# A recurrent pipeline over four engines: one sum and the shifted variances on VectorE, a new order on TensorE and ScalarE, two buffers for a tanh

## The chip, the core and the metric

The program runs on one core of a Trainium2 chip. The core has TensorE (PE in the profile) for matrix products and transposes, VectorE (DVE), ScalarE (ACT) and GpSimd (POOL) for the rest, and queues that start DMAs. Each engine runs its own list of instructions in order, and the lists meet only at semaphores. The metric is the time of one whole execution on the device, in microseconds, and less is better.

## What is computed

The program is a chain of four sub-layers on 32 sequences of 256 tokens with 128 features, in float32. The change lies in the third, which is a recurrent mixing layer followed by a gated feed-forward layer:

```python
def _wkv(k, v, time_decay, time_first):       # a scan along the tokens
    ew = jnp.exp(-jnp.exp(time_decay))
    def step(carry, kv):
        a, b = carry
        ek = jnp.exp(kv[0])
        a = ew * a + ek * kv[1]
        b = ew * b + ek
        return ((a, b), a / (b + WKV_EPS))
...
xn = _ln(x, ln1_g, ln1_b)
xp = _shift(xn)                               # the token before
k = (xn * mix_k + xp * (1.0 - mix_k)) @ Wk
v = (xn * mix_v + xp * (1.0 - mix_v)) @ Wv
r = jax.nn.sigmoid((xn * mix_r + xp * (1.0 - mix_r)) @ Wr)
wkv = _wkv(k, v, time_decay, time_first)
x = x + r * wkv @ Wo
yn = _ln(x, ln2_g, ln2_b)
yp = _shift(yn)
kk = jnp.square(jax.nn.relu((0.5 * yn + 0.5 * yp) @ Wfk))
rr = jax.nn.sigmoid(yn @ Wfr)
return x + rr * (kk @ Wfv)
```

The layer's input is a normalised sum of the sub-layer before, whose expert outputs are gathered by token here, and its own output is added to `x` and normalised again. `_ln` needs a mean and a variance over the 128 features of each token.

## The kernel before

`build` runs the stages one after the other, each in a block of its own that ends on all engines before the next begins. The change is in `recur` (L1645), which takes the 32 sequences, called t, through a pipeline of stages. Every engine has the same loop `for i in turns` (i from -3 to 39), and in turn i it works on several sequences at once, each a fixed number of turns older: in the middle of the stage GpSimd gathers for i+3, VectorE sums and measures i+1, TensorE turns i, the scans work on i-1, `output` on i-2, the second normalisation on i-3, `keys` on i-4 and `values` on i-5. `live(t)` says whether a sequence is in 0 to 31. The order of an engine's work in a turn is the order of the calls in its loop, written by hand. `wait_past(engine, semaphore, n)` waits where n is positive.

What a turn does on each engine, in its order before the change:

- TensorE (L1791): `keys(i-4)` multiplies `both` by `w_k` in eight matmuls into two `key_bank`s; `project(i-1)` makes key and value in `kv_bank` and the first gate in the left half of `gate_bank` from `xn`; `output(i-2)`; `turn(i)` transposes `z` once it is there; `turn_second(i-3)` transposes `z2`; `values(i-5)`; `receptance(i-4)` makes the second gate in the right half of `gate_bank`.
- ScalarE (L1888): `exponents(i-1)` writes `e_k` from the key bank; `normalise_second(i-3)` and `normalise_first(i)` write `z2` and `z` with the scales in `roots` and the offsets in `shifts`; `rectify(i-4)` reads the key banks; `affine_second(i-3)` writes `yn`; `add_eps(i-1)` writes `b_eps`; `gate(i-1)` is the first tanh; `square(i-4)`; `affine(i)` writes `xn`; `normalise_row(i)`; `normalise_third(i-7)` writes `fresh`; `gate_second(i-4)` is the second tanh, into the one buffer `half_tanh2`.
- VectorE (L2042): `shift(i-1)` writes `shifts` once GpSimd has made `roots`; then means and variances of `total` (`aggregate(2)`), `weigh` (`ekv`), the two gathered sums, the two scans, `add_output`, the spreads, the reciprocal (L1996), the last `moments` (two `aggregate`s, four instructions at L1947), `double` (L2026), `gate_second` (L2015), `divide` (L2002), `add_second` (L2022), `gate` (L2008) and the spread of `total` (L1941).
- GpSimd (L2116): two gathers, `add_old(i-3)` (L2113), which writes `both` as the sum of `yn` and `yn` one token earlier, a third gather, `scale(i)` and the fourth gather. `scale` waits for the `moments` of the turn, adds the epsilons to the variances in two small instructions (`bases`, L2104 and L2105) and raises ten numbers a partition to the power -1/2 (`roots`, L2108).

The semaphores that matter: `moments_done` lets `scale` begin, `rooted` lets `shift` begin, `shifted` lets ScalarE normalise, `both_ready` lets `keys` begin, `yn_ready` lets `both` be made, `gated2_done` frees `half_tanh2` and half of `out_bank`.

## Time and profile before

| what | value |
|---|---|
| median of 3 runs | 2475.6 us (2472.62 to 2476.64) |
| the profiled execution | 2475.63 us |
| its span, first to last instruction | 2473.9 us |
| granted TensorE clock, mean of the span | 0.891 |
| the recurrent stage | 1214 to 1549 us |
| a turn in its middle | 8.96 us |
| busy over the span: PE, DVE, ACT, POOL | 79%, 62%, 52%, 42% |

In a row of a timeline the first number is the start, the second the length, and a bracket at the end gives the idle time of that engine before it and what ended it. Two instructions of the same kind that follow each other are one row with x2. The lengths of neighbours overlap a little, so what an instruction costs its engine is the distance to the next start. Instructions that start DMAs or only wait are not counted as busy, except GpSimd's indirect gathers.

### The profile page before, as it was taken

Reading aid. Unit: us, or ns where it says so; the run is one execution under the profiler, and the core shown is the slowest. Engines: PE = TensorE matmul, PEld = TensorE weight load, DVE = VectorE, ACT = ScalarE, POOL = GpSimd, SP = SyncE. Lnnn points to the kernel's source line nnn. Section 1 sums busy time; section 2 is a strip of 40 time slices with the busy share of each in tenths; the row PEclk is TensorE's granted clock in tenths of the full one; section 3 lists DMA queues with packets and bytes.
Section 4 is the critical chain, followed back from the end, with each engine's and each line's share of the span. In section 5 each row is a group of like instructions: output and inputs, shape, how many; then the busy total and the mean of one; then the engine's idle time right before and its main releaser. Section 6 shows DMA issues by size and latency. Waiting matters only on the chain. (4 is left out here: it accounts for less than half of the span.)

```text
span 2473.9 us, 52699 instructions
## 1 busy us (share of the span) xinstructions
PE 1946.5 (79%) x16756; PEld 1600.7 (65%) x16788; DVE 1531.0 (62%) x6215; ACT 1275.3 (52%) x3105; POOL 1046.7 (42%) x1285
## 2 busy tenths in 40 slices
PE   7799999999997897999578888599998758856610
PEld 6455555555555886877467777488887757755500
DVE  2478788888886583421279997588887564313345
ACT  3588888888884322333258887344443104423310
POOL 2133333333331315555478885222222115566654
PEclk9799999999998898999889999799999559977655
DMA  7799999999995104555412221000001115533323
GB/s 237 254 313 311 312 311 317 313 311 312 312 313 164 56 1 124 154 154 151 108 29 58 60 60 44 18 1 2 1 1 30 74 34 155 155 114 110 101 73 74
DMA packets 198092, 353.95 MB, mean 143 GB/s; under 512 B 25280, under 2 KB 145856, under 8 KB 196800
## 3 DMA queue, kind: packets, MB, share of 16 engines
q1 hardware_dynamic: 140752, 294.77, 36.6%
q0 software_dynamic: 17664, 36.21, 6.2%
q10 hardware_dynamic: 39408, 19.60, 2.7%
q8 instruction: 143, 2.34, 0.4%
q14 instruction: 125, 1.02, 0.1%
HBM read 165.87 MB, written 145.52 MB: 126 GB/s over the span
## 5 line engine op out<-in xcount | busy, mean ns | idle before, releaser
L1389 POOL DMA_INDIRECT moe_route_rows_sb<-tokens,moe_taken x296 | 279.8, 945 | 291.7 <-PE moe_route_bank L1429 145.6
L177 POOL TENSOR_SCALAR_AFFINE_SELECT heads_raw_relative<-heads_raw_relative 128x508 f32<-128x508 f32 x256 | 166.7, 675 | 500.8 <-ACT heads_raw_relative L562 460.9
L1547 DVE COPY moe_route_y<-moe_route_bank 128x128 f32<-128x128 f32 x296 | 86.1, 291 | 427.3 <-PE moe_route_bank L1448 218.9
L1488 ACT COPY moe_route_rows_t<-moe_route_bank 128x128 f32<-128x128 f32 x296 | 78.4, 265 | 435.0 <-PE moe_route_bank L1429 270.1
L1438 PE MATMUL moe_route_bank<-moe_route_rows_t,moe_route_w_now 128*128 128x128 f32 x1184 | 220.9, 315 | 85.7 <-issue 74.9
L562 ACT COPY heads_raw_relative<-heads_rel_bank 128x768 f32<-128x768 f32 x247 | 198.7, 804 | 125.6 <-PE heads_rel_bank L457 125.5
L1448 PE MATMUL moe_route_bank<-moe_w,moe_route_hid 128*128 x1184 | 218.9, 312 | 47.3 <-issue 24.8
L486 PE MATMUL attend_turn_bank<-ident,attend_score 128*128 128x128 f32 x1536 | 232.0, 287 | 20.5 <-ACT attend_prob_t L568 19.2
L1438 PEld LDWEIGHTS moe_route_bank<-moe_route_rows_t,moe_route_w_now 128*128 128x128 f32 x1184 | 180.3, 217 | 103.8 <-issue 98.9
L486 PEld LDWEIGHTS attend_turn_bank<-ident,attend_score 128*128 128x128 f32 x1536 | 163.8, 142 | 117.5 <-ACT attend_prob_t L568 68.1
L568 ACT ACTIVATE attend_prob_t<-attend_turn_bank 128x384 f32<-128x384 f32 x512 | 224.8, 500 | 6.9 <-PE attend_turn_bank L486 6.9
L1448 PEld LDWEIGHTS moe_route_bank<-moe_w,moe_route_hid 128*128 128x128 f32 x1184 | 175.2, 212 | 72.4 <-issue 65.8
L572 ACT ACTIVATE attend_score<-attend_score,attend_extreme 128x128 f32<-128x128 f32 x512 | 215.7, 421 | 9.1 <-DVE attend_extreme L619 8.8
L619 DVE CUSTOM_DVE_ANT_0 attend_score<-attend_score_bank,heads_relative 128x256 f32<-128x256 f32 x512 | 214.5, 419 | 0.0
L625 DVE TENSOR_SCALAR attend_score<-attend_score,attend_extreme 128x256 f32<-128x256 f32 x512 | 195.2, 381 | 0.0
L616 DVE CUSTOM_DVE_ANT_0 attend_score<-attend_score_bank,heads_relative 128x128 f32<-128x128 f32 x512 | 146.2, 285 | 78.4 <-PE attend_score_bank L457 52.6
L2229 POOL TENSOR_TENSOR batch_prob<-batch_e_x,batch_recip 128x512 f32<-128x512 f32 x64 | 67.1, 1048 | 234.4 <-DVE batch_recip L2446 234.4
L457 PE MATMUL attend_score_bank<-heads_qk 32*128 32x256 f32 x1024 | 156.1, 381 | 0.0
L457 PE MATMUL heads_rel_bank<-heads_e,heads_qk 32*128 32x256 f32 x988 | 150.8, 382 | 0.0
L2092 POOL DMA_INDIRECT recur_got<-expert_out,moe_slots x128 | 136.8, 1068 | 32.1 <-issue 32.1
L1382 POOL DMA_INDIRECT moe_route_got<-expert_out,moe_slots x128 | 121.7, 951 | 65.2 <-issue 40.9
L454 PE MATMUL heads_rel_bank<-heads_e,heads_qk 32*128 32x128 f32 x988 | 122.9, 325 | 21.2 <-PEq L59 3.2
(321 smaller groups left out, 5072.4 us busy)
## 6 DMA issues: line engine op xcount, KB each, us to landing
shear<-heads_raw_relative SPq DMA_DIRECT2D x128, 768.0 KB, 5.5
heads_relative<-shear SPq DMA_DIRECT2D x128, 768.0 KB, 6.4
moe_route_w_now<-moe_w SPq DMA_DIRECT2D x296, 129.0 KB
expert_out<-moe_route_y ACTq DMA_DIRECT2D x73, 256.0 KB
qk_heads<-project_qk SPq DMA_DIRECT2D x32, 256.0 KB, 4.3
heads_qk<-qk_heads SPq DMA_DIRECT2D x128, 64.0 KB
tokens<-moe_z SPq DMA_DIRECT2D x8, 1024.0 KB, 4.1
moe_route_rows_sb<-tokens,moe_taken POOLq DMA_INDIRECT x296
```

The costliest lines, as they stand in the source:

```text
L177: m = nc.gpsimd.affine_select(out=future, in_=future, compare_op=ALU.is_ge, fill=-BIG, base=1 - P, pattern=[[0, QUAD], [1, P - 1]], channe ...
L457: mm = nc.tensor.matmul(bank[:, P:W], q[:, P:T], m[:, P:W] if of_rel else m[:, 0:T], start=True, stop=True)
L486: mm = nc.tensor.transpose(bank[:, j * P:(j + 1) * P], score[:, (h - LAG) % RING, j * P:(j + 1) * P], c.ident[:, :])
L562: nc.scalar.copy(raw[:, ring, 2 * half:2 * half + 2, :], r_bank[:, :, 0:W]).then_inc(rel_moved, 1)
L568: nc.scalar.activation(prob_t[:, (h - LAG) % RING, :], bank_of(h)[:, 0:W], ACT.Exp).then_inc(exped, 1)
L572: nc.scalar.activation(score[:, h % RING, 0:P], score[:, h % RING, 0:P], ACT.Identity, bias=extreme[:, h % RING, 0:1], scale=-1.0).then_in ...
L616: nc.vector.tensor_tensor_reduce(score[:, row, 0:P], bank[:, 0:P], rel[:, quad, h % QUAD, 0:P], -SM_SCALE, 3.0e38, ALU.add, ALU.min, extre ...
L619: nc.vector.tensor_tensor_reduce(score[:, row, P:W], bank[:, P:W], rel[:, quad, h % QUAD, P:W], SM_SCALE, -3.0e38, ALU.add, ALU.max, extre ...
L625: nc.vector.tensor_scalar(score[:, h % RING, P:W], score[:, h % RING, P:W], extreme[:, h % RING, 1:2], None, ALU.subtract).then_inc(centre ...
L1389: nc.gpsimd.indirect_dma_start(rows_sb[:, s % TAKEN, :], None, c.tokens, bass.IndirectOffsetOnAxis(ex.taken[:, s // S, s % S:s % S + 1], 0 ...
L1438: mm = nc.tensor.matmul(hid_bank[u][:, k * P:(k + 1) * P], w1_now[r][:, k * P:(k + 1) * P], rows_t[u][:, :], start=True, stop=True)
L1448: mm = nc.tensor.matmul(y_bank[:, 0:D], hid[u][:, k, :], w, start=k == 0, stop=k == 1)
```

## The change

Four things change, all in `recur`.

`add_old` moves from GpSimd to VectorE, behind `divide`. The two instructions for `bases` move to VectorE as `shift_variances`, behind `double`, and `scale` on GpSimd now waits for them and makes only `roots`. On VectorE `gate_second` also moves, from behind `double` to behind `gate`, directly ahead of `add_second`. On TensorE `keys` moves from the head of the turn to behind `output`, and on ScalarE the first tanh and `add_eps` move ahead of `rectify`, the tanh first. `half_tanh2` gets two buffers. The semaphore `halved` takes over the start-up part of `based`.

```diff
-        half_tanh2, gated2 = sb("half_tanh2", [P, T]), sb("gated2", [P, T])
+        half_tanh2, gated2 = [sb(f"half_tanh2_{u}", [P, T]) for u in range(2)], sb("gated2", [P, T])
...
             for i in turns:
-                if live(i - 4):
-                    keys(i - 4)
                 if live(i - 1):
                     project(i - 1)
                 if live(i - 2):
                     output(i - 2)
+                if live(i - 4):
+                    keys(i - 4)
                 if live(i):
                     turn(i)
...
             def gate_second(t):
                 act.wait_ge(r2_made, t + 1)
-                wait_past(act, gated2_done, t)
-                nc.scalar.activation(half_tanh2[:, :], gate_bank[:, T:2 * T], ACT.Tanh, scale=0.5).then_inc(tanhed2, 1)
+                wait_past(act, gated2_done, t - 1)
+                nc.scalar.activation(half_tanh2[t % 2][:, :], gate_bank[:, T:2 * T], ACT.Tanh, scale=0.5).then_inc(tanhed2, 1)
...
                 if live(i):
                     normalise_first(i)
+                if live(i - 1):
+                    gate(i - 1)
+                    add_eps(i - 1)
                 if live(i - 4):
                     rectify(i - 4)
                 if live(i - 3):
                     affine_second(i - 3)
-                if live(i - 1):
-                    add_eps(i - 1)
-                    gate(i - 1)
...
+            def add_old(t):
+                dve.wait_ge(yn_ready, t + 1)
+                wait_past(dve, k_made, 2 * t - 2)
+                nc.vector.tensor_tensor(both[t % 2][:, :], yn[t % 2][:, 1:], yn[t % 2][:, 0:T], ALU.add).then_inc(both_ready, 1)
+
+            def shift_variances(turn):
+                u = turn % 2
+                dve.wait_ge(moments_done, moments_made(turn))
+                wait_past(dve, rooted, scales_made(turn - 2))
+                nc.vector.tensor_scalar(bases[u][:, 0:3, :], moments[u][:, :, :, 1], 1.0, LN_EPS, ALU.mult, ALU.add)
+                nc.vector.tensor_scalar(bases[u][:, 3:5, :], moments[u][:, 0::2, :, 1], 1.0 + LN_EPS, LN_EPS ** 2, ALU.mult, ALU.add
+                                        ).then_inc(based, 1)
...
                 if live(i - 5):
                     double(i - 5)
-                    gate_second(i - 5)
+                if i in scaled:
+                    shift_variances(i)
                 if live(i - 1):
                     divide(i - 1)
-                if live(i - 5):
-                    add_second(i - 5)
+                if live(i - 3):
+                    add_old(i - 3)
                 if live(i - 1):
                     gate(i - 1)
                 if live(i - 5):
+                    gate_second(i - 5)
+                    add_second(i - 5)
                     dve.wait_ge(totalled, i - 4)
                     spread(2, i - 5, total[(i - 5) % SUMS])
...
             def scale(i):
                 u = i % 2
-                pool.wait_ge(moments_done, moments_made(i))
+                pool.wait_ge(halved, 1)
+                pool.wait_ge(based, scales_made(i))
...
-                nc.gpsimd.tensor_scalar(bases[u][:, 0:3, :], moments[u][:, :, :, 1], 1.0, LN_EPS, ALU.mult, ALU.add).then_inc(based, 1)
-                nc.gpsimd.tensor_scalar(bases[u][:, 3:5, :], moments[u][:, 0::2, :, 1], 1.0 + LN_EPS, LN_EPS ** 2, ALU.mult, ALU.add
-                                        ).then_inc(based, 1)
-                pool.wait_ge(based, 2 * scales_made(i) + 1)
                 nc.gpsimd.tensor_tensor(roots[u][:, :, :], bases[u][:, :, :], minus_half[:, :, :], ALU.pow).then_inc(rooted, 1)
...
-            def add_old(t):
-                pool.wait_ge(yn_ready, t + 1)
-                wait_past(pool, k_made, 2 * t - 2)
-                nc.gpsimd.tensor_tensor(both[t % 2][:, :], yn[t % 2][:, 1:], yn[t % 2][:, 0:T], ALU.add).then_inc(both_ready, 1)
...
-                if live(i - 3):
-                    add_old(i - 3)
```

TensorE, a turn in the middle of the stage; `key_bank` is written by `keys`, `kv_bank` by `project`, `out_bank` by `output` (L1751) and `values` (L1787), `turn_bank` by the two transposes:

```order
 L1743 MATMUL recur_gate_bank<-recur_xn,recur_w_old 128x256
 L1751 MATMUL recur_out_bank<-recur_w_out,recur_gated 128x128 x2
+L1767 MATMUL recur_key_bank<-recur_both,recur_w_k 128x256 x4
 L1730 MATMUL recur_turn_bank<-ident,recur_z 128x128 x2
 L1759 MATMUL recur_turn_bank<-ident,recur_z 128x128 x2
 L1787 MATMUL recur_out_bank<-recur_w_v,recur_kk 128x128 x8
 L1777 MATMUL recur_gate_bank<-recur_w_r,recur_yn 128x128 x2
-L1767 MATMUL recur_key_bank<-recur_both,recur_w_k 128x256 x4
 L1742 MATMUL recur_kv_bank<-recur_xn,recur_w_now 128x256
```

`keys` has gone from ahead of the projections to behind `output`, ahead of the transpose that waits for `z`.

VectorE before, from the reciprocal to the `shifts` of the next turn; `recur_gated` at L2015 is the second gate, at L2008 the first:

```order
L1996 RECIPROCAL recur_b_inv<-recur_b_eps 128x256
L1947 BN_AGGR recur_moments<-recur_stats 128x2 x4
L2026 TENSOR_TENSOR recur_total<-recur_x_2,rows 128x256
L2015 SCALAR_TENSOR_TENSOR recur_gated<-recur_half_tanh,recur_out_bank 128x256
L2002 TENSOR_TENSOR recur_ratio<-recur_scan_a,recur_b_inv 128x256
L2022 TENSOR_TENSOR recur_total<-recur_total,recur_gated 128x256
L2008 SCALAR_TENSOR_TENSOR recur_gated<-recur_half_tanh,recur_ratio 128x256
L1941 BN_STATS recur_stats<-recur_total 128x6 x2
L1953 SCALAR_TENSOR_TENSOR recur_shifts<-recur_moments,recur_roots 128x6
```

VectorE now, the same stretch (line numbers are those of the changed kernel; L2028 is the second gate, L2021 the first):

```order
L2009 RECIPROCAL recur_b_inv<-recur_b_eps 128x256
L1947 BN_AGGR recur_moments<-recur_stats 128x2 x4
L2039 TENSOR_TENSOR recur_total<-recur_x_1,rows 128x256
L1988 TENSOR_SCALAR recur_bases<-recur_moments 128x6
L1989 TENSOR_SCALAR recur_bases<-recur_moments 128x4
L2015 TENSOR_TENSOR recur_ratio<-recur_scan_a,recur_b_inv 128x256
L1982 TENSOR_TENSOR recur_both<-recur_yn 128x256
L2021 SCALAR_TENSOR_TENSOR recur_gated<-recur_half_tanh,recur_ratio 128x256
L2028 SCALAR_TENSOR_TENSOR recur_gated<-recur_half_tanh_1,recur_out_bank 128x256
L2035 TENSOR_TENSOR recur_total<-recur_total,recur_gated 128x256
L1941 BN_STATS recur_stats<-recur_total 128x6 x2
L1953 SCALAR_TENSOR_TENSOR recur_shifts<-recur_moments,recur_roots 128x6
```

The two `bases` and `both` are new in the row, and the second gate now stands directly ahead of the add that reads it.

GpSimd before, a turn:

```order
L2108 TENSOR_TENSOR recur_roots<-recur_bases,recur_minus_half 128x10
L2092 DMA recur_got<-expert_out,moe_slots 128x128 x3
L2113 TENSOR_TENSOR recur_both<-recur_yn 128x256
L2092 DMA recur_got<-expert_out,moe_slots 128x128
L2104 TENSOR_SCALAR recur_bases<-recur_moments 128x6
L2105 TENSOR_SCALAR recur_bases<-recur_moments 128x4
```

GpSimd now, two turns and the start of a third:

```order
L2121 TENSOR_TENSOR recur_roots<-recur_bases,recur_minus_half 128x10
L2108 DMA recur_got<-expert_out,moe_slots 128x128 x4
L2121 TENSOR_TENSOR recur_roots<-recur_bases,recur_minus_half 128x10
L2108 DMA recur_got<-expert_out,moe_slots 128x128 x4
L2121 TENSOR_TENSOR recur_roots<-recur_bases,recur_minus_half 128x10
```

Only the gathers and `roots` are left there.

## Rows read from the trace of the kernel before

**Rows 1.** By stretch: busy us (instructions) of PE, PEld, DVE, ACT, POOL; then granted clock.
```profile
1380.00:1420.00 40.00, 36.01 (x212) 31.85 (x213) 35.98 (x135) 32.62 (x80) 33.97 (x37) 1.00 0.26 60
```

**Rows 2.** Waits, 1262 to 1500 us: who waited for whom, us in total, times, longest.
```profile
ACT recur_e_k L1825 <- PE recur_kv_bank L1743: 42.5, 26, 4.6
...
DVE recur_shifts L1953 <- POOL recur_roots L2108: 23.6, 26, 2.2
...
DVE recur_ekv L1972 <- ACT recur_e_k L1826: 2.6, 2, 1.3
```

**Rows 3.** Timeline of VectorE, one turn; start, length, instruction, idle before.
```profile
1392.89 0.17 DVE L1953 SCALAR_TENSOR_TENSOR recur_shifts<-recur_moments,recur_roots 128x6 f32<-128x6 f32 x1 [0.81 <-POOL recur_roots L2108]
1392.97 0.16 DVE L1955 SCALAR_TENSOR_TENSOR recur_shifts<-recur_moments,recur_roots 128x2 f32<-128x2 f32 x1
...
1398.68 0.32 DVE L1947 BATCH_NORM_AGGREGATE recur_moments<-recur_stats 128x2 f32<-128x6 f32 x4
1398.91 0.39 DVE L2026 TENSOR_TENSOR recur_total<-recur_x,rows 128x256 f32<-128x256 f32 x1
1399.22 0.41 DVE L2015 SCALAR_TENSOR_TENSOR recur_gated<-recur_half_tanh,recur_out_bank 128x256 f32<-128x256 f32 x1
...
1399.89 0.43 DVE L2022 TENSOR_TENSOR recur_total<-recur_total,recur_gated 128x256 f32<-128x256 f32 x1
1400.24 0.41 DVE L2008 SCALAR_TENSOR_TENSOR recur_gated<-recur_half_tanh,recur_ratio 128x256 f32<-128x256 f32 x1
1400.57 0.47 DVE L1941 BATCH_NORM_STATS2 recur_stats<-recur_total 128x6 f32<-128x128 f32 x2
1401.85 0.17 DVE L1953 SCALAR_TENSOR_TENSOR recur_shifts<-recur_moments,recur_roots 128x6 f32<-128x6 f32 x1 [0.80 <-POOL recur_roots L2108]
```

**Rows 4.** Timeline of GpSimd, the same turn.
```profile
1397.12 0.62 POOL L2113 TENSOR_TENSOR recur_both<-recur_yn 128x256 f32<-128x256 f32 x1
...
1399.09 0.28 POOL L2104 TENSOR_SCALAR recur_bases<-recur_moments 128x6 f32<-128x6 f32 x1 [0.23 <-DVE recur_moments L1947]
...
1399.72 2.10 POOL L2108 TENSOR_TENSOR recur_roots<-recur_bases,recur_minus_half 128x10 f32<-128x10 f32 x1
```

**Rows 5.** Timeline of TensorE, the same turn and the next.
```profile
1397.79 2.00 PE L1767 MATMUL recur_key_bank<-recur_both,recur_w_k 128*128 128x256 f32 x8
1399.62 0.59 PE L1742 MATMUL recur_kv_bank<-recur_xn,recur_w_now 128*128 128x256 f32 x2
...
1403.82 0.44 PE L1730 MATMUL recur_turn_bank<-ident,recur_z 128*128 128x128 f32 x2 [1.00 <-ACT recur_z L1817]
```

**Rows 6.** Timeline of ScalarE, the turn after.
```profile
1401.55 0.26 ACT L1825 ACTIVATE recur_e_k<-recur_kv_bank,recur_cols 128x1 f32<-128x1 f32 x1 [1.44 <-PE recur_kv_bank L1743]
...
1402.12 0.88 ACT L1817 ACTIVATE recur_z<-recur_x,recur_shifts,recur_roots 128x128 f32<-128x128 f32 x2
...
1406.69 0.56 ACT L1874 ACTIVATE recur_xn<-recur_turn_bank,recur_cols 128x256 f32<-128x256 f32 x1
```

**Rows 7.** Timeline of VectorE, tail of the stage.
```profile
1530.83 0.42 DVE L2015 SCALAR_TENSOR_TENSOR recur_gated<-recur_half_tanh,recur_out_bank 128x256 f32<-128x256 f32 x1 [3.16 <-issue]
1531.29 0.42 DVE L2022 TENSOR_TENSOR recur_total<-recur_total,recur_gated 128x256 f32<-128x256 f32 x1
1531.75 0.48 DVE L1941 BATCH_NORM_STATS2 recur_stats<-recur_total 128x6 f32<-128x128 f32 x2
```

**Rows 8.** The line that makes roots; ns shortest/median/longest, first and last start us.
```profile
L2108 POOL TENSOR_TENSOR recur_roots<-recur_bases,recur_minus_half x39: 1952/2094/2104, 1230.2 to 1545.5; 128x10 f32<-128x10 f32 x39
```

**Rows 9.** Timeline of GpSimd, first and last steady turn, one of the tail.
```profile
1283.44 2.10 POOL L2108 TENSOR_TENSOR recur_roots<-recur_bases,recur_minus_half 128x10 f32<-128x10 f32 x1
...
1498.48 2.10 POOL L2108 TENSOR_TENSOR recur_roots<-recur_bases,recur_minus_half 128x10 f32<-128x10 f32 x1
...
1534.78 0.61 POOL L2113 TENSOR_TENSOR recur_both<-recur_yn 128x256 f32<-128x256 f32 x1 [3.24 <-ACT recur_yn L1853]
...
1536.03 1.96 POOL L2108 TENSOR_TENSOR recur_roots<-recur_bases,recur_minus_half 128x10 f32<-128x10 f32 x1
```

More of the change, by code:

```diff
@@ L1685, in recur @@
         stats_done = [sem(f"stats_done{k}") for k in range(3)]
-        half_summed, summed, row_ready, moments_done, based, rooted, shifted, ratio2_done, rest_done = (
-            sem(x) for x in ("half_summed", "summed", "row_ready", "moments_done", "based", "rooted", "shifted", "ratio2_done", "rest_done"))
+        half_summed, summed, row_ready, moments_done, based, halved, rooted, shifted, ratio2_done, rest_done = (
+            sem(x) for x in ("half_summed", "summed", "row_ready", "moments_done", "based", "halved", "rooted", "shifted", "ratio2_done", "rest_done"))
         gathered = c.indirect["moe0_gathered"]
@@ L2014, in gate_second @@
                 wait_past(dve, totalled, t)
-                nc.vector.scalar_tensor_tensor(out=gated2[:, :], in0=half_tanh2[:, :], scalar=1.0, in1=out_bank[:, T:T + BLK * D],
+                nc.vector.scalar_tensor_tensor(out=gated2[:, :], in0=half_tanh2[t % 2][:, :], scalar=1.0, in1=out_bank[:, T:T + BLK * D],
                                                op0=ALU.add, op1=ALU.mult).then_inc(gated2_done, 1)
@@ L2103, in scale @@
                 wait_past(pool, rest_done, upto(i - 8))
-                nc.gpsimd.tensor_scalar(bases[u][:, 0:3, :], moments[u][:, :, :, 1], 1.0, LN_EPS, ALU.mult, ALU.add).then_inc(based, 1)
-                nc.gpsimd.tensor_scalar(bases[u][:, 3:5, :], moments[u][:, 0::2, :, 1], 1.0 + LN_EPS, LN_EPS ** 2, ALU.mult, ALU.add
-                                        ).then_inc(based, 1)
-                pool.wait_ge(based, 2 * scales_made(i) + 1)
                 nc.gpsimd.tensor_tensor(roots[u][:, :, :], bases[u][:, :, :], minus_half[:, :, :], ALU.pow).then_inc(rooted, 1)
-            def add_old(t):
-                pool.wait_ge(yn_ready, t + 1)
-                wait_past(pool, k_made, 2 * t - 2)
-                nc.gpsimd.tensor_tensor(both[t % 2][:, :], yn[t % 2][:, 1:], yn[t % 2][:, 0:T], ALU.add).then_inc(both_ready, 1)
-            nc.gpsimd.memset(minus_half[:, :, :], -0.5).then_inc(based, 1)
+            nc.gpsimd.memset(minus_half[:, :, :], -0.5).then_inc(halved, 1)
             for i in turns:
```

## The prediction

> **What bounds the kernel now.** The change touches only the recurrent stage, from 1214 to 1549 us of a span of 2473.9 us. The stage is a block of its own, so what it loses or gains counts in full. I read the busy table by stretch first [rows 1]: in the middle of the stage all four engines are 82 to 90% busy and TensorE's granted clock is 1.00. Nothing is far ahead, so a ring of waits sets the period of a turn. The list of waits over 26 turns [rows 2] shows that each waits for another once a turn: ScalarE 1.6 us on the mean for the key and value projections, VectorE 0.9 for `roots`. The timelines say which of these is the ring.
>
> VectorE [rows 3]: `shifts` starts at 1392.89 and again at 1401.85, a period of 8.96. Between them VectorE works to the spread of `total`, which starts 7.68 in, then waits 0.80 for `roots`. The last `moments` end at 1399.00. GpSimd [rows 4]: the two `bases` start at 1399.09, `roots` at 1399.72, and `roots` ends at 1401.82, 0.03 before `shifts`. So the ring is: VectorE from `shifts` to the end of `moments` 6.11, wake 0.09, `bases` 0.63, `roots` 2.10, wake 0.03, together 8.96. Two others lie close behind. GpSimd alone is idle 0.23 before `bases`, so it could turn in about 8.75. For TensorE and ScalarE [rows 5, 6]: TensorE idles 1.00 for `z` ahead of `turn`, so its own work is 7.96; ScalarE starts `z` 0.57 after `e_k` (two instructions), about 0.1 later than instructions of that length need, which is the slack of that ring.
>
> **What leaves the ring.** The two `bases` leave GpSimd, 0.63 a turn, and `both` too, 0.62 and what stands behind it [rows 4]. GpSimd then needs about 7.6 a turn and is no bound. Against that, VectorE now runs `double` and the two new instructions before `roots` can start. Back to back, a VectorE instruction costs 0.07 to 0.09 less than its length: `shifts` is 0.17 long and its successor starts 0.08 later, `add_second` 0.43 long and the next starts 0.35 later [rows 3]. So `double`, 0.39 long, costs 0.31. The new two have 6 and 4 elements a partition, and no row shows them on VectorE. The nearest is `shifts`, same engine and size: 0.08 a step, 0.15 to 0.17 long [rows 3]. On GpSimd they took 0.28 and together 0.63 [rows 4], the dear end. I take 0.08 each, the row of the same engine. The ring becomes 6.02 to the start of `double`, 0.31, 0.08, 0.15 for the second to end, wake 0.09, `roots` 2.10, wake 0.03: 8.78.
>
> **What fills VectorE.** Its work before is 7.68 to the last spread and 0.40 for it: 8.08. Added are the two small ones, 0.16, and `both`, a 128x256 add of two SBUF inputs, whose like are `double` at 0.31 and `add_second` at 0.35 [rows 3], so 0.33 (0.62 on GpSimd is the other end [rows 4]). The new order also puts three dependent instructions in a row: second gate, add, spread. In the tail of the stage the same three run so, with steps of 0.46 and 0.46 [rows 7]; in the middle of the old order the second gate costs 0.33 and the add 0.35 [rows 3]: 0.24 more. The sum is 8.08 + 0.16 + 0.33 + 0.24 = 8.81. That is just above the ring: VectorE itself is late next, and the period is **8.81** against 8.96.
>
> One rule speaks against exactly this move. Rows first: `add_second` at 1399.89 and `gate` at 1400.24 each read two SBUF tensors, start while `roots` (1399.72 to 1401.82) reads SBUF on GpSimd, and take 0.43 and 0.41, about as much as `double` at 0.39, which runs before `roots` [rows 3, 4]. The Trainium skill (SBUF — State Buffer, Who interferes with whom) says that such a pair exclude each other: whoever starts second is blocked until the other ends. By the rows the sum stands at 8.81 a turn; by that rule it would be the lock rival below, 10.74.
>
> **The new order on TensorE and ScalarE** gives nothing by itself in the middle, but the move needs it. `both` now starts 6.8 after `shifts` (6.33 to the small ones, 0.16, divide 0.34) and ends at 7.2; `keys` began at 1397.79, 4.9 after `shifts`, and `project` at 1399.62 [rows 5]. With `keys` still ahead, the projections would wait 2.3. In the new order TensorE projects as soon as `xn` is there: ScalarE has the same instructions between `z` and `xn`, so `xn` is done 5.1 after `z` starts (1402.12 to 1406.69 and 0.56) [rows 6], 5.4 after `shifts`. Projections, gate and `output` take 3.2 (1399.62 to 1403.82 less 1.00), so to 8.6; `keys` take 1.83 more (1397.79 to 1399.62), to 10.5, that is 1.7 into the next turn, while `z` is done at 1.97 of it (1403.82 against 1401.85). So 0.2 to 0.3 remains of TensorE's 1.0 idle. The key and value banks are made 1.9 after `project` starts (1399.62 to `e_k` at 1401.55), at 7.3, and ScalarE's own work ends at about 7.2. ScalarE gets `keys` late as well; it fills the time with the first tanh and `b_eps` and rectifies at about 2.5, by when half of `keys` is made. `add_old` makes VectorE wait for `yn`, with `gate`, the second gate, spread and `shifts` queued behind it; `yn` comes before `xn`, so before 5.4, and is asked for at 6.8. The second `half_tanh2` buffer lets ScalarE write the next tanh while VectorE's second gate, now later, reads the last one; with one buffer `e_k` would stand behind that wait. The cover of all this is VectorE's full row.
>
> **The stage's turns.** `roots` runs 39 times, from 1230.2 to 1545.5, so there are 38 intervals [rows 8]: 6 of ramp up to 1283.44 (53.3 us), 24 steady to 1498.48 (215.0 us, 8.96 each) and 8 of tail (47.1 us) [rows 9].
> Steady: 24 x 0.15 = **3.6** us.
> Ramp: in the first four intervals the `bases` go from GpSimd's chain, 0.63 [rows 4] against about 0.1 to 0.2 on VectorE; I count 0.5 each, 2.0. The last two are the longest, 10.2 and 9.9: there `keys` stands before `project`, and VectorE waits for `e_k` twice, 2.6 in all, 1.3 at most [rows 2]. With `project` ahead those 1.3 go, and 0.45 of `bases`: 1.75 each, 3.5. Ramp: **5.5**, between 2 (only `bases`) and 7.
> Tail: once no gathers are left, `roots` queues on GpSimd behind `both`, which waits 3.24 for `yn`: from the start of `both` at 1534.78 to `roots` at 1536.03 are 1.25 [rows 9]. In the new order `roots` does not wait for `both`. I count 1.25 for two intervals and 0.3 for the three before them, 3.4; the last three may grow as `values` catch up, and I take 0.4 back. Tail: **3.0**, between 0 and 5.
> Sum: 3.6 + 5.5 + 3.0 = **12.1**. The profiled execution took 2475.63 us with a span of 2473.9, the same as the median of the runs, so the sum is taken from 2475.6: **2463.5 us**. With the terms at their ends (steady 0 to 5 by the price of the small ones) it is 2458.6 to 2473.6.
>
> **Rivals.**
> *VectorE is full already.* If its additions cost 0.15 more a turn (0.16 each for the small ones do that), the steady turn stays 8.96 and ramp and tail alone gain 8.5: 2467. For: VectorE is within hundredths of the ring, and no row shows it reading `moments` in steps. Against: `shifts` reads them so. 15%.
> *Ramp and tail give little.* The first turns wait on something else than `keys`, and in the tail `values` takes the place of `both`: 2, 0 and steady 2 to 3, 2471. Against: the 2.6 of waiting for `e_k` is in the trace. 10%.
> *The moved instructions keep GpSimd's price* (slower). VectorE would pay 0.63 for the small ones and 0.78 for `both` with its wait, 0.92 more than I charged: a turn of 9.73, 24 x 0.77 = 18.5 lost, 8.5 gained in ramp and tail: 2485.6. It decides from 0.15 extra a turn, turns the sign at 0.5 and passes 0.2% at 0.7. Every VectorE row of the two sizes speaks against. 9%.
> *The lock.* `both`, at 6.83, would be held by `roots` to 8.76, and after it run `gate`, second gate, add and spread: 0.33 + 0.33 + 0.46 + 0.46 + 0.40, a turn of 10.74; 24 x 1.78 = 42.7 lost and 8.5 back, 2509.8. The 0.43 and 0.41 above speak against. 3%. This is the rule of the Trainium skill named above.
> *More than forecast.* `roots` shrinks from 2.10 to the 1.95 of its shortest [rows 8] and VectorE hides the dependent steps: 8.65 a turn, tail 5: 2457.6. 8%.
> The forecast keeps 55%.
>
> **How the numbers follow.** A measurement of this kernel tells 0.2%, about 5 us, from no change. Faster by more: the forecast, the last case, most of the first and a little of the second, 0.74. Within: 0.14. Slower: the third and fourth, 0.12. The range 2457 to 2474 leaves out those 0.12 and about 0.06 of still larger gains.
>
> **What would show it.** In the profile after: `roots` to `roots` 8.81 in the middle; VectorE's wait for `roots` from 0.8 to under 0.1; steps of 0.08 for the small ones and 0.46 from second gate to add and to spread; GpSimd idle about 1.1 before `roots`; TensorE's wait for `z` 0.2 to 0.3; no wait of `ekv` for `e_k` in the ramp. I am wrong if VectorE waits for `yn`, if TensorE waits for `both`, or if `both` or `gate` lasts over 0.5 under `roots`.

## The result and the profile after

| | before | changed |
|---|---|---|
| median of 19 runs each | 2475.6 us (2469.38 to 2487.28) | 2481.65 us (2471.99 to 2491.88) |
| profiled execution, its span | 2475.63, 2473.9 us | 2483.72, 2482.0 us |
| first to last `roots`, 38 turns | 315.4 us | 318.6 us |
| a turn in the middle | 8.96 us | 9.44 us |

The ratio is 1.0028, 95% interval 1.0018 to 1.0037: slower by 0.3%, where 12 us of gain were forecast. The stage lost 3.2 us in the profiled executions. The other 4.9 us of the two spans lie mostly behind the last `roots` (933.0 against 928.3 us), almost all of it in stages that were not changed; a second profile of the changed kernel, below, has 929.4 there. So 3.2 is what the change did, and the rest of the 6 us between the medians has no place in the code that these runs show.

The line that makes `roots`, answering [rows 8] (ns shortest/median/longest, first and last start in us):

```profile
L2121 POOL TENSOR_TENSOR recur_roots<-recur_bases,recur_minus_half x39: 1954/2702/2713, 1230.4 to 1549.0; 128x10 f32<-128x10 f32 x39
```

The median has gone from 2.09 to 2.70 us, with the same instruction, operands and engine. Its shortest is still 1.95. The timeline of VectorE and GpSimd together, one turn in the middle, answering [rows 3, 4] (start, length, engine, instruction, idle before):

```profile
1390.50 0.32 DVE L1947 BATCH_NORM_AGGREGATE recur_moments<-recur_stats 128x2 f32<-128x6 f32 x4
1390.73 0.39 DVE L2039 TENSOR_TENSOR recur_total<-recur_x,rows 128x256 f32<-128x256 f32 x1
1391.04 0.16 DVE L1988 TENSOR_SCALAR recur_bases<-recur_moments 128x6 f32<-128x6 f32 x1
1391.11 0.16 DVE L1989 TENSOR_SCALAR recur_bases<-recur_moments 128x4 f32<-128x4 f32 x1
1391.18 0.42 DVE L2015 TENSOR_TENSOR recur_ratio<-recur_scan_a,recur_b_inv 128x256 f32<-128x256 f32 x1
1391.41 2.70 POOL L2121 TENSOR_TENSOR recur_roots<-recur_bases,recur_minus_half 128x10 f32<-128x10 f32 x1 [1.22 <-issue]
1391.52 0.42 DVE L1982 TENSOR_TENSOR recur_both<-recur_yn 128x256 f32<-128x256 f32 x1
1391.85 0.42 DVE L2021 SCALAR_TENSOR_TENSOR recur_gated<-recur_half_tanh,recur_ratio 128x256 f32<-128x256 f32 x1
1392.19 0.41 DVE L2028 SCALAR_TENSOR_TENSOR recur_gated<-recur_half_tanh,recur_out_bank 128x256 f32<-128x256 f32 x1
1392.63 0.42 DVE L2035 TENSOR_TENSOR recur_total<-recur_total,recur_gated 128x256 f32<-128x256 f32 x1
1393.09 0.49 DVE L1941 BATCH_NORM_STATS2 recur_stats<-recur_total 128x6 f32<-128x128 f32 x2
1394.15 0.17 DVE L1953 SCALAR_TENSOR_TENSOR recur_shifts<-recur_moments,recur_roots 128x6 f32<-128x6 f32 x1 [0.57 <-POOL recur_roots L2121]
```

Read the starts: the small instructions cost 0.07 each, `both` 0.33 (1391.52 to 1391.85), the second gate 0.44 and the add 0.46, all as forecast. None of VectorE's instructions under `roots` is longer than 0.42. Only `roots` is long, and VectorE idles 0.57 for it. The ring is now 6.02 + 0.31 + 0.07 + 0.30 (1391.11 to 1391.41, of it 0.14 of wake) + 2.71 + 0.03 = 9.44.

The waits of 1262 to 1500 us, answering [rows 2] (who waited for whom, us in total, times, longest):

```profile
ACT recur_z L1817 <- DVE recur_shifts L1955: 39.9, 26, 1.7
...
PE recur_turn_bank L1730 <- ACT recur_z L1817: 18.2, 24, 0.8
...
DVE recur_shifts L1953 <- POOL recur_roots L2121: 15.5, 25, 1.2
ACT recur_e_k L1825 <- PE recur_kv_bank L1743: 12.4, 26, 3.1
```

The first three hang on the ring: VectorE waits 0.6 a turn for `roots`, ScalarE 1.5 for `shifts`, TensorE 0.8 for `z`. The wait of `ekv` for `e_k`, 2.6 before, is gone, and in this stretch no engine waits for `both` or `yn`.

By stretch of the stage: the ramp's six turns take 47.6 us (53.3 before), the 24 of the middle 226.1 (215.0), the tail's eight 44.8 (47.1). That is 5.6 and 2.2 won and 11.1 lost. The length of `roots` goes with it: 1.99 to 2.04 in the ramp, 2.70 or 2.71 in 23 turns of the middle (2.41 and 2.16 in two), 1.95 to 2.01 in the late tail.

### The profile page after: what moved, and what is told of

It reads as the page before. It is cut to its first block and busy times, and to the rows that moved or that the text cites. A ratio compares the mean times of both kernels' runs of the same rounds, so it can differ in the third digit from the quotient of the medians.

```text
span 2482.0 us, 52771 instructions
## 1 busy us (share of the span) xinstructions
PE 1950.0 (79%) x16756; PEld 1594.0 (64%) x16788; DVE 1553.7 (63%) x6325; ACT 1276.8 (51%) x3105; POOL 1025.2 (41%) x1175
## 3 DMA queue, kind: packets, MB, share of 16 engines
q8 instruction: 143, 2.34, 0.4%
```

## Experiments

The expectations call the explanations by letters. P: `roots` is held back while VectorE runs instructions with two SBUF inputs one behind the other. L: it is long because VectorE is busy during all of it (the load). W: it is long because GpSimd has idled and wakes, or because VectorE has just written its operands. T, which comes later: any run of full-size VectorE instructions holds it, and only something about the second gate ends that. "The small two" are the two `bases`.

The experiments are told in the order in which they ran. Each edit is against the changed kernel unless it says otherwise. The table has the length of `roots` and the turn in the middle, the 38 turns, and the ratio to the kernel before, with its interval where there were several runs. The first four ran on a chip on which the kernel before took 2352.5 us, so their times compare only as ratios; the turns of the stage compare all the same, since the one with the old GpSimd and VectorE code has 8.96 and 2.10 there too.

| experiment | `roots` | turn | 38 turns | ratio to before |
|---|---|---|---|---|
| second gate first | 1.98 | 8.72 | 303.0 | 0.9939 (0.9924 to 0.9954) |
| `both` back on GpSimd | 2.04 | 8.77 | 302.2 | 0.9934 (0.9920 to 0.9949) |
| `bases` back on GpSimd | 1.98 | 8.96 | 311.0 | 0.9985 (0.9975 to 0.9995) |
| orders only | 2.10 | 8.96 | 311.5 | 0.9981 (0.9972 to 0.9990) |
| changed kernel again | 2.71 | 9.44 | 318.5 | 1.0016 (1.0000 to 1.0032) |
| hide and shorten | 1.98 | 8.68 | 302.7 | 0.9954 (0.9936 to 0.9972) |
| longer run | 2.03 | 8.88 | 304.8 | 0.9966 (0.9948 to 0.9984) |
| pause of 32 | 2.04 | 8.78 | 303.3 | one run: 2464.14 against 2472.06 us |
| pause of 96 | 2.08 | 8.81 | 303.1 | one run: 2456.05 against 2474.56 us |
| `both` from one input | 2.03 | 8.77 | 303.7 | one run: 2459.36 against 2474.56 us |
| keys ahead | 2.70 | 11.22, 12.89 | 401.9 | 1.0354 (1.0332 to 1.0376) |
| one tanh buffer, pause of 32 | 2.04 | 8.78 | 306.5 | one run: 2466.1 against 2474.56 us |
| first gate from one input | 2.37 | 9.10 | 310.4 | one run: 2469.15 against 2472.53 us |
| second gate from two inputs | 3.04 | 9.78 | 327.0 | one run: 2483.7 against 2472.53 us |

**Second gate first.** It is the one whose bank operand lies in PSUM; it now stands between the `bases` and `divide`.

```diff
                     shift_variances(i)
+                if live(i - 5):
+                    gate_second(i - 5)
                 if live(i - 1):
                     divide(i - 1)
...
                 if live(i - 5):
-                    gate_second(i - 5)
                     add_second(i - 5)
```

> The changed kernel with one call moved: on VectorE the second gate runs directly behind the two small instructions, ahead of divide, both and the first gate, all of which read two SBUF tensors; the second gate reads one SBUF tensor and PSUM. Theory P (roots, which reads SBUF on GpSimd, is held back by VectorE instructions with two SBUF inputs that follow each other without a gap): with the second gate under the start of roots it lasts about 2.0 us as in the ramp instead of 2.70, a turn takes 6.02+0.31+0.08+0.30+2.0+0.03 = 8.74 us, and the whole about 2462. Rival L (roots is long because VectorE works through the whole of it, with no idle time left): order changes nothing, roots 2.7, a turn 9.44, the whole about 2481. Rival W (roots is long because GpSimd has idled and wakes, or because its operands were just written by VectorE): also 2.7 and 2481.

Both numbers came (1.98 and 8.72), and L and W had said 2.7. Nothing was taken from VectorE or GpSimd, only the neighbour of `roots` changed, and 0.72 of 9.44 is gone: 0.72 of `roots` itself. One turn of the middle is an exception: at 1308.76 us `roots` starts 0.34 later against VectorE, behind the second gate, with `divide`, `both`, the first gate and the add in a row, and takes 3.07.

**`both` back on GpSimd**, in its old place between the second and the third gather of a turn:

```diff
-                nc.vector.tensor_tensor(both[t % 2][:, :], yn[t % 2][:, 1:], yn[t % 2][:, 0:T], ALU.add).then_inc(both_ready, 1)
...
+                nc.gpsimd.tensor_tensor(both[t % 2][:, :], yn[t % 2][:, 1:], yn[t % 2][:, 0:T], ALU.add).then_inc(both_ready, 1)
```

> The changed kernel with only both returned to GpSimd, at its old place behind the second gather. VectorE then has divide, gate, second gate under the start of roots. Theory P: the run of two-SBUF instructions is one shorter, roots gets in at the second gate at the latest, 0.33 earlier: 2.0 to 2.4 us, a turn of 8.75 to 9.1, the whole 2462 to 2471. Rival L: VectorE has 0.33 less work under roots and idles that long, so roots shrinks a little at most, 2.5 to 2.7, a turn 9.25 to 9.4. Rival W: 2.7 and 9.44.

Without `both` between them there is a gap between `divide` and the first gate, which needs the result of `divide` (it starts 0.51 after it, not 0.33), and `roots` is short. So it isn't the new place of `bases` by itself that makes `roots` long.

**`bases` back on GpSimd**, as in the kernel before, with `both` still on VectorE:

```diff
-                if i in scaled:
-                    shift_variances(i)
...
+                nc.gpsimd.tensor_scalar(bases[u][:, 0:3, :], moments[u][:, :, :, 1], 1.0, LN_EPS, ALU.mult, ALU.add).then_inc(based, 1)
```

> The changed kernel with only the two bases returned to GpSimd, both stays on VectorE. roots starts 6.83 us after shifts, while VectorE runs both, then the first gate (two SBUF inputs each), then the second gate (PSUM). Theory P: roots lasts 2.1 if it gets in between both and the first gate, 2.45 if only at the second gate; a turn 8.96 to 9.31. Rival L: VectorE works under all of roots, 2.7, a turn 9.56. Rival W: GpSimd runs without a pause and made the operands itself, so 1.95 to 2.1, a turn 8.96.

`roots` starts 0.4 later against VectorE: `both` is running since 0.28, the first gate follows 0.06 later, and `roots` takes 1.98. `both` alone doesn't make it long either; it is where `roots` falls. By itself this run doesn't speak for P: W had named just these numbers (1.95 to 2.1 and 8.96) and P 2.1 at the least. What speaks against W is its 2.7 for the two runs before.

**Orders only**: the kernel before with the new order on TensorE and ScalarE and the two tanh buffers.

> The kernel before with the new order on TensorE and ScalarE and the two tanh buffers, nothing moved between engines. Step of the prediction on trial: the orders are worth nothing in the middle (a turn stays 8.96, roots 2.10) and take out the two 1.3 us waits for e_k in the ramp: the whole about 2473. Rival: they are worth more or cost in the middle, if TensorE and ScalarE were the ring: over 1 per mille either way, a turn other than 8.9 to 9.0.

The middle doesn't move, as the prediction had it; the stage is 3.9 us shorter, in the last turns of the ramp (9.09 and 8.52 for 10.18 and 9.91) and in the tail.

**The changed kernel again.**

> The changed kernel itself, unaltered, on the chip and beside the runs of the kernel before that the experiments have. Every theory: roots 2.70 in the middle, a turn 9.44, 2 to 4 per mille slower than before. If instead roots is 2.0 here, the 2.70 was a matter of the chip and not of the order.

The same turns and lengths, so they belong to the program. The ratio is below the 2 to 4 per mille expected, but its interval overlaps that of the first comparison.

**Hide and shorten**: the second gate directly behind the `bases`, `double` behind `divide`, `both` behind `add_second`, where it fills the gap ahead of the spread.

```diff
                     shift_variances(i)
+                if live(i - 5):
+                    gate_second(i - 5)
                 if live(i - 1):
                     divide(i - 1)
-                if live(i - 3):
-                    add_old(i - 3)
+                if live(i - 5):
+                    double(i - 5)
                 if live(i - 1):
                     gate(i - 1)
                 if live(i - 5):
-                    gate_second(i - 5)
                     add_second(i - 5)
+                if live(i - 3):
+                    add_old(i - 3)
```

> The changed kernel with VectorE's order: the small two directly behind moments, second gate, divide, double, first gate, add_second, both, spread of total. Theory P (roots is held back by VectorE instructions with two SBUF inputs run back to back, unless one with PSUM stands at its start): roots 1.98. double leaves the ring: 8.72 - 0.31 + 0.05 for the wait on moments = 8.46, so VectorE's own work binds, 8.57 + 0.05 = 8.62 a turn; against the kernel with only the second gate moved 24 x 0.10 = 2.4 us less, in all 0.7 per cent below the kernel before. Rival L (load under roots counts, not the order): roots 2.7, a turn 9.1.

8.68, a little over the 8.62 expected. In the middle (1276 to 1500 us) the list of waits has none of VectorE for `roots`: VectorE is the bound now. The whole came out at 0.9954, short of the 0.7 per cent expected. Its interval and that of "second gate first" overlap, so which of the two is the better version is open; both beat both kernels.

**Longer run**: `double` behind the first gate, so that four instructions with two SBUF inputs stand in a row.

```diff
-                if live(i - 5):
-                    double(i - 5)
...
                 if live(i - 5):
+                    double(i - 5)
                     gate_second(i - 5)
```

> The changed kernel with double moved behind the first gate: the small two, divide, both, first gate, double, then second gate. The run of back to back two-SBUF instructions ahead of the first one with PSUM is 0.33 longer. Theory P: roots gets in only at the second gate and lasts 2.70 + 0.33 = 3.03, a turn of 6.11 + 0.05 + 0.08 + 0.30 + 3.03 + 0.03 = 9.60. Rival L or W: roots stays 2.70, a turn 9.27.

All theories missed. The timeline of the two engines:

```profile
1371.31 0.42 DVE L2015 TENSOR_TENSOR recur_ratio<-recur_scan_a,recur_b_inv 128x256 f32<-128x256 f32 x1
1371.55 2.03 POOL L2120 TENSOR_TENSOR recur_roots<-recur_bases,recur_minus_half 128x10 f32<-128x10 f32 x1 [1.05 <-issue]
1371.65 0.43 DVE L1982 TENSOR_TENSOR recur_both<-recur_yn 128x256 f32<-128x256 f32 x1
1372.00 0.41 DVE L2021 SCALAR_TENSOR_TENSOR recur_gated<-recur_half_tanh,recur_ratio 128x256 f32<-128x256 f32 x1
1372.33 0.41 DVE L2039 TENSOR_TENSOR recur_total<-recur_x,rows 128x256 f32<-128x256 f32 x1
```

`roots` starts under `divide` with `both` 0.10 behind, as in the changed kernel (0.11), and yet takes 2.03. `both` is 0.01 longer and its successor comes 0.35 after it, not 0.33. It looks as if `roots` had slipped in between `divide` and `both`, at a cost of 0.01 to 0.02 to VectorE. So a row of such instructions doesn't always keep `roots` out, and P as first put is too strong. That takes away two causes: VectorE is as busy as in the changed kernel, and `roots` starts 0.15 after the end of `bases` (0.14 there), so neither load nor the wake sets the length.

**Pause of 32**: a memset that nobody needs, between the `bases` and `divide`.

```diff
+        pause = sb("pause", [P, 32])
...
+                    nc.vector.memset(pause[:, :], 0.0)
```

> The changed kernel with one memset of 32 elements a partition (about 0.05 us) between the small two and divide; it writes a tile that nobody reads, and puts divide, both and gate 0.05 us later against the start of roots. In the ramp and the tail of the changed kernel roots took 2.03 with both at 0.10 or 0.11 after its start, and in the kernel before 2.10 with the next instruction at 0.17. Theory P with a gap that must fall at the right moment: roots 2.0 to 2.15, a turn 8.8 to 8.9. Theory P without that (a run is never broken): 2.75, a turn 9.5. Rival L: 2.70 to 2.75.

A useless instruction makes the turn 0.66 shorter. `both` now comes 0.12 after the start of `roots`, a hundredth later than without the pause. Its 38 turns are the answer to the prediction's sum: with `roots` let in, the same work takes 303.3 us, 12.1 less than the kernel before; 12.1 were forecast, though not in these parts (see below).

**Pause of 96**, the same with 96 elements.

> The changed kernel with one memset of 96 elements a partition, about 0.10 to 0.12 us in place of the 0.03 that 32 elements cost, between the small two and divide. In the runs so far the length of roots is 1.93 plus the offset at which a VectorE instruction's place becomes free: 0.11 gives 2.04, 0.17 gives 2.10, 0.78 gives 2.70. With both at about 0.20 to 0.23 that makes 2.13 to 2.16 and a turn of 8.87 to 8.90. If roots loses at both and gets in at the first gate, 2.5; at the second gate, 2.8.

The pause cost 0.06 rather than 0.10 to 0.12. `both` stands at 0.16 and `roots` takes 2.08: 0.04 later, 0.04 longer.

**`both` from one input**: it is made from `yn` alone, so the sum with the token before is left out.

```diff
-                nc.vector.tensor_tensor(both[t % 2][:, :], yn[t % 2][:, 1:], yn[t % 2][:, 0:T], ALU.add).then_inc(both_ready, 1)
+                nc.vector.tensor_scalar(both[t % 2][:, :], yn[t % 2][:, 1:], cols[:, 0:1], cols[:, 1:2], ALU.mult, ALU.add).then_inc(both_ready, 1)
```

> The changed kernel, in which both is made by a tensor_scalar from yn alone (the sum with the token before is left out, so the feed-forward part computes something else); place, size and semaphores of the instruction stay. It reads one SBUF tensor, apart from two columns. Theory P (only instructions with two SBUF inputs keep roots out): roots gets in where both starts, 0.11 after its own start, and lasts 1.93 + 0.11 = 2.04, a turn 8.78. Rival T (any run of full-size VectorE instructions holds it, and only the second gate's wait or its PSUM input ends it): 2.70 and 9.44.

The order, the length (0.40) and the place of `both` are those of the changed kernel; its second SBUF input is gone (and the operation is another for it), and with it the 0.66. One turn goes against P:

```profile
1348.42 0.41 DVE L1982 TENSOR_SCALAR recur_both<-recur_yn,recur_cols 128x256 f32<-128x256 f32 x1
1348.61 2.39 POOL L2121 TENSOR_TENSOR recur_roots<-recur_bases,recur_minus_half 128x10 f32<-128x10 f32 x1 [1.52 <-issue]
1348.74 0.42 DVE L2021 SCALAR_TENSOR_TENSOR recur_gated<-recur_half_tanh,recur_ratio 128x256 f32<-128x256 f32 x1
1349.07 0.42 DVE L2028 SCALAR_TENSOR_TENSOR recur_gated<-recur_half_tanh,recur_out_bank 128x256 f32<-128x256 f32 x1
```

The one-input `both` is already running when `roots` starts, as the second gate is in "second gate first", and yet `roots` takes 2.39, as if it got in only at the second gate (0.46 after its start).

**Keys ahead**: `keys(i - 4)` back at the head of TensorE's turn.

> The changed kernel with keys back at the head of TensorE's turn. The step of the prediction on trial: the projections then wait behind keys for both. both ends about 7.2 after shifts, keys to 9.0, key and value banks at 10.95, e_k and ekv at 11.5 where VectorE wants them 0.4 after the next shifts: a turn of about 11.1 against 9.44, so about 40 us more than the changed kernel, 2515. Rival: TensorE has idle time enough, under 5 us more.

The timeline of TensorE, and after it the waits of 1300 to 1500 us:

```profile
1391.71 2.70 PE L1767 MATMUL recur_key_bank<-recur_both,recur_w_k 128*128 128x256 f32 x8 [2.35 <-DVE recur_both L1982]
1394.21 1.06 PE L1742 MATMUL recur_kv_bank<-recur_xn,recur_w_now 128*128 128x256 f32 x2
...
1396.52 0.59 PE L1743 MATMUL recur_kv_bank<-recur_xn,recur_w_old 128*128 128x256 f32 x2
```

```profile
PE recur_key_bank L1767 <- DVE recur_both L1982: 37.7, 16, 2.5
```

TensorE waits 2.35 for `both`; the prediction said 2.3. That makes 11.22. Every other turn or so is 12.89: there the pairs of matmuls behind the wait take 1.06 in place of 0.59, and the mean granted clock from 1391.7 to 1396.0 is 0.63, so part of it ran at the lower level, 1.2 GHz; from 1396.5 it is 1.00 again. TensorE had run nothing for 2.35 us ahead of that stretch. In the next turn the wait is as long (2.34, to 1404.61) and the clock behind it stays at 1.00. All 24 turns of the middle sort that way: in about the first 4.3 us behind the wait the clock is 0.61 to 0.70 in the 13 turns of 12.6 to 12.9, and 1.00 in the 11 of 11.2 to 11.6. Where it falls it costs 1.67 on top, which the expectation left out: hence 2562 us where 2515 were expected.

**One tanh buffer**: the pause of 32 with one `half_tanh2` and the wait of the kernel before.

```diff
-        half_tanh2, gated2 = [sb(f"half_tanh2_{u}", [P, T]) for u in range(2)], sb("gated2", [P, T])
+        half_tanh2, gated2 = [sb(f"half_tanh2_{u}", [P, T]) for u in range(1)] * 2, sb("gated2", [P, T])
...
-                wait_past(act, gated2_done, t - 1)
+                wait_past(act, gated2_done, t)
```

> The kernel with the 32-element pause (a turn of 8.78) with one half_tanh2 buffer instead of two. The second gate ends about 7.9 after shifts, so the second tanh starts at 7.95 instead of 6.8 and e_k at 8.25. z waits for shifts until 9.05, which covers it: a turn stays 8.78 and the buffer was worth nothing. Rival, as the prediction put it: e_k stands behind the wait and the turn grows, 9.0 or more.

The turn stays 8.78. ScalarE waits for the second gate 17 times, 0.9 on the mean, and it is hidden. Four turns in the middle of this one run are longer (9.43, 9.73, 9.12, 11.53), and with them the 38 turns take 3.2 more than with the pause alone. ScalarE doesn't wait for the second gate in them (1333 to 1374 us); whether the buffer makes them by another way is open.

**First gate from one input**, the rest as in the changed kernel: it is made from `ratio` alone, the tanh factor is left out.

```diff
-                nc.vector.scalar_tensor_tensor(out=gated[t % 2][:, :], in0=half_tanh[t % 2][:, :], scalar=1.0, in1=ratio[:, :],
-                                               op0=ALU.add, op1=ALU.mult).then_inc(gated_done, 1)
+                nc.vector.tensor_scalar(gated[t % 2][:, :], ratio[:, :], cols[:, 0:1], cols[:, 1:2], ALU.mult, ALU.add).then_inc(gated_done, 1)
```

> The changed kernel, in which the first gate is made by a tensor_scalar from ratio alone (the tanh factor is left out), so that it reads one SBUF tensor; both still reads two. roots starts 0.10 before both and 0.44 before the first gate. Theory P (roots waits while two-SBUF instructions follow each other and gets in at the first place taken by another): 1.93 + 0.44 = 2.37, a length that no run has shown yet, and a turn of 9.11. Rival T (what lets roots in is something of the second gate: its PSUM input or the wait on the run of instructions): 2.70 and 9.44. A third outcome, 2.04, would say that the place at both is won or lost by luck of the timing, as with the pause.

```profile
1386.06 0.41 DVE L2015 TENSOR_TENSOR recur_ratio<-recur_scan_a,recur_b_inv 128x256 f32<-128x256 f32 x1
1386.29 2.37 POOL L2120 TENSOR_TENSOR recur_roots<-recur_bases,recur_minus_half 128x10 f32<-128x10 f32 x1 [1.23 <-issue]
1386.40 0.41 DVE L1982 TENSOR_TENSOR recur_both<-recur_yn 128x256 f32<-128x256 f32 x1
1386.73 0.40 DVE L2021 TENSOR_SCALAR recur_gated<-recur_ratio,recur_cols 128x256 f32<-128x256 f32 x1
1387.06 0.41 DVE L2027 SCALAR_TENSOR_TENSOR recur_gated<-recur_half_tanh,recur_out_bank 128x256 f32<-128x256 f32 x1
```

The run of instructions with two SBUF inputs ends at the gate, 0.44 after `roots` starts, and `roots` takes 2.37. T had 2.70.

**Second gate from two inputs**: it reads the decay row in SBUF in place of `out_bank` in PSUM, so the product with `values` is left out.

```diff
-                nc.vector.scalar_tensor_tensor(out=gated2[:, :], in0=half_tanh2[t % 2][:, :], scalar=1.0, in1=out_bank[:, T:T + BLK * D],
+                nc.vector.scalar_tensor_tensor(out=gated2[:, :], in0=half_tanh2[t % 2][:, :], scalar=1.0, in1=decay_row[:, :],
```

> The changed kernel, in which the second gate reads decay_row, a tensor in SBUF of the same size, in place of its PSUM bank (the feed-forward value is left out). The run divide, both, first gate, second gate is then four instructions of two SBUF inputs, and add_second, which depends on the last, starts after a gap at 1.22. Theory P: roots gets in when the second gate's place is over, 0.78 + 0.33 = 1.11, and lasts 3.04, a turn of 9.78. Rival T, if it is the wait at 0.78 and not the PSUM input that lets roots in: 2.70 and 9.44. Rival L (load only): 2.70.

```profile
1385.44 3.04 POOL L2121 TENSOR_TENSOR recur_roots<-recur_bases,recur_minus_half 128x10 f32<-128x10 f32 x1 [1.23 <-issue]
1385.55 0.41 DVE L1982 TENSOR_TENSOR recur_both<-recur_yn 128x256 f32<-128x256 f32 x1
1385.89 0.41 DVE L2021 SCALAR_TENSOR_TENSOR recur_gated<-recur_half_tanh,recur_ratio 128x256 f32<-128x256 f32 x1
1386.22 0.41 DVE L2028 SCALAR_TENSOR_TENSOR recur_gated<-recur_half_tanh,recur_decay_row 128x256 f32<-128x256 f32 x1
1386.67 0.42 DVE L2035 TENSOR_TENSOR recur_total<-recur_total,recur_gated 128x256 f32<-128x256 f32 x1
```

Now the second gate belongs to the run. It starts 0.78 after `roots`, and one step of 0.33 further, at 1.11, the run ends, since the add has to wait for the gate's result. `roots` takes 3.04, with the same VectorE lengths of 0.41. The second gate's place and kind of instruction are the same here; only where it reads its second input from has changed.

## Why the prediction was wrong

**The cause.** `roots` is held up, most likely where it takes its operands, while VectorE runs instructions with two inputs in SBUF back to back. It gets in where one with a PSUM input or a single SBUF input stands, or a gap, and in some kernels already at the boundary between two of the row ("before", "longer run" and the pauses in the table). Its length is 1.93 plus the distance from its start to that place; 1.93 is what fits all rows:

| kernel | `roots` gets in at | after its start | 1.93 + that | measured |
|---|---|---|---|---|
| second gate first | second gate, already running | no distance | - | 1.98, as with VectorE idle in the ramp of before |
| longer run, `both` from one input | `both` | 0.10 | 2.03 | 2.03 |
| pause of 32 | `both` | 0.12 | 2.05 | 2.04 |
| pause of 96 | `both` | 0.16 | 2.09 | 2.08 |
| before | `add_second` [rows 3, 4] | 0.17 | 2.10 | 2.10 |
| first gate from one input | first gate | 0.44 | 2.37 | 2.37 |
| changed | second gate | 0.78 | 2.71 | 2.70 |
| second gate from two inputs | behind the second gate | 1.11 | 3.04 | 3.04 |

The last two experiments were foretold to the hundredth from this. The odd turns fit too: in the changed kernel `roots` takes 2.41 at 1353.70, where the second gate comes 0.48 after its start, and 2.16 at 1429.18, where `both` comes 0.24 after it; in "second gate first" the row ends 1.15 after the start of the long one, 3.08 for the 3.07 measured. In the changed kernel `divide`, `both` and the first gate form the run, and `roots` starts 0.23 after `divide`. The price is 2.70 less 2.04, 0.66 a turn: 9.44 in place of 8.78.

**The step that failed** is the term `roots` 2.10 in the ring, kept from before. The step that priced the pair looked at the wrong side: it asked whether `both` and the gate would be held up by `roots`, found them at 0.41 to 0.43, and concluded that there is no contention. They are held by 0.03 at most; `roots` is held by up to 0.66 more. The rows of before could have told it: the same instruction takes 1.95 at its shortest and 2.10 in the middle [rows 8], where `divide` and `add_second` stand around its start.

The Trainium skill (SBUF — State Buffer, Who interferes with whom) names this pair: a VectorE instruction with two SBUF inputs, and a GpSimd instruction that reads SBUF. The two kernels with an input taken away agree (2.03 and 2.37 for 2.70), and so does its rule that the one which comes second is blocked, once it is seen that `divide` was running before `roots`. That the owner keeps the ports for its whole instruction, as it says too, is not what the rows show of GpSimd as the owner: `both`, `gate` and `double` run at 0.41 to 0.43 while `roots` is at work for 2 us, and `roots`, once in, needs the same 1.93 in every row of the table. It seems to need them only while it reads ten numbers a partition; no run here shows that moment by itself.

**Point by point.**
- *The ring.* Right but for `roots` and 0.05 of wake (0.14 for 0.09). With `roots` let in by the pause, the turn is 8.78 for 8.81, and VectorE waits for `roots` once, 0.2, from 1290 to 1490: it is full, as forecast.
- *The signs of being wrong.* None came: no wait for `yn` or `both`, nothing over 0.42 under `roots`. They watched the engine that was given the work and not the length of `roots`.
- *VectorE's steps* 0.07, 0.33, 0.44 and 0.46: right. So the first rival falls, and the one with GpSimd's prices, though its 2485.6 is the nearest to the result.
- *The orders* give nothing in the middle: right (orders only). With `keys` ahead TensorE waits 2.35 for 2.3: right.
- *Ramp* 5.6 for 5.5: right; the orders alone give 2.5 of it, for the 2.6 of waiting for `e_k`. *Tail* 2.2 for 3.0: short, since `roots` still takes 2.70 and 2.67 in its first two turns; with the pause it wins 3.5. Its working, `roots` queueing behind `both`, holds only in part: the tail takes 45.7 with the orders only (1.4 of gain), 44.0 with `both` moved as well and 44.1 with the `bases` moved in its place.
- *The second buffer*: not borne out. With one, 20 of the 24 turns are the same.
- *TensorE's wait for `z`*, 0.8 for 0.2 to 0.3, is the longer ring.
- *The lock*, 3%: right in kind, wrong in who waits and how long. It should have been two rivals. The one in which GpSimd waits for the end of the run makes the ring 0.66 longer, 9.44 where VectorE's 8.81 was the bound: 2475.6 - 12.1 + 24 x 0.63 = 2478.6. It had no chance of its own.
- *The sum*: with the pause 12.1 for 12.1, but as ramp 4.4, middle 4.2 and tail 3.5 for 5.5, 3.6 and 3.0. That the three errors cancel is luck.

**What stays open** is why `roots` sometimes gets in between two neighbours of the run and sometimes not. Between `divide` and `both` it does at 0.10 to 0.12 in the ramp and the tail, the longer run and the pause, and doesn't at 0.10 to 0.11 in the middle of the changed kernel and in the last two experiments. Between `both` and the gate it does at 0.05 with the `bases` back on GpSimd and at 0.15 in one turn of the longer run, and doesn't at 0.15 in one turn each of the changed kernel and of "keys ahead" (2.41). In the kernel before it always gets in between `divide` and the add, at 0.17. These distances overlap, so the distance alone doesn't decide it; what the pause changes besides a hundredth of a us is not known. Nor is it known why the running one-input `both` didn't let it in (2.39). Within a program it repeats: the second profile has the same turns.

## What to carry to other kernels

When one engine's instruction on the critical ring changes its length between stretches of a trace, find what runs beside it at its start before keeping its length in a sum. VectorE work with two SBUF inputs is best not put in a row ahead of a GpSimd instruction that others wait for: one instruction with a PSUM or single input at that place was enough here, in all but one of the 24 turns of "second gate first", and an order that has it costs nothing. Of two engines that may hold each other, price both sides; the one that starts second is not always the one that you moved.

## What the runs showed of the hardware

- GpSimd's `roots`, 128x10, takes 1.95 us with VectorE idle in the late tail (1.98 to 1.99 in the ramp) and 3.04, once 3.07, beside a run of VectorE instructions with two SBUF inputs; VectorE loses 0.01 to 0.03.
- A memset of 128x32 ahead of the run, which shifts `both` by 0.01, takes 0.66 off a turn.
- VectorE's `bases` step on by 0.07 for 6 and 4 elements a partition, against 0.63 for both on GpSimd [rows 4].
- After TensorE had stood still for 2.35 us the granted clock was 0.63 on the mean of the next 4.3 us in one turn, and 1.00 after the same wait in the next ("keys ahead", where 13 of 24 turns have the low one).
